# First attention, values' product: one block of 512 queries every second step in place of two halves in neighbouring steps

## The chip, the cores and the metric

One core of one Trainium2 chip runs the whole program. The metric is the device time of one execution in microseconds; three runs of the kernel before are given, and the hardware profiler took one more execution, whose trace is read below.

## What is computed

The program is a two-layer network on 16 groups of 512 tokens with 128 features. The change touches the attention of layer 0 alone:

```
x = x + proj(softmax(q k^T / sqrt(8)) v)      # 16 groups, 16 heads of 8 features, 512 tokens each
    q, k, v = split(layernorm(x) @ qkv_w + qkv_b)
```

Around it stand, in this order: the first mixture-of-experts feed-forward of layer 0 (its names begin with ffnA), this attention (att), the second feed-forward (ffnB), and layer 1 with a kernelized attention and a spline feed-forward (att1k, att1q). The attention must not start before ffnA is done, and ffnB starts when it has ended.

## The kernel before

`attn0` runs a software pipeline over 16 groups with 32 steps for each. A group has 4 units of 4 heads each, and a unit has 4 key tiles of 128 keys. Step k of the pipeline handles one key tile of one pair of heads, so that a unit takes 8 steps, and a key tile takes 2.

In every step PE, which works strictly in program order, issues up to three things:

- `again(k)`, the transposed scores "t": keys of one tile by 512 queries for two heads, two fp32r matmuls of 26 rows into one of the banks `att_pair` (L957). ACT takes the exponential of it (`exps`, L873) into `att_pt`.
- `scores(k + 43)`, the scores "s" that only serve to find the row maxima, two matmuls of 24 rows (L947). DVE reduces them (`maxed`, L698). They run 43 steps ahead of t.
- `weigh`, the product with the values "W" (L969): `att_pt` of a key tile for the four heads of the unit, against the values, into the bank `att_o`. Four fp32 matmuls stand side by side, one for each head, on 32 columns of the array each; the trace shows two instructions for each.

`att_pair` has three banks that t and s take in turn (t, s, t, s, ...). So a t must wait until DVE has reduced the s issued three uses before, and an s until ACT has taken the exponential of the t issued three uses before, which is the t of the step before. `att_pt` has 8 buffers.

`weigh` is cut into two halves of 256 queries, and the table WEIGHED says in which step of the unit (and of its follower) each half is issued: steps 4, 5, 6, 7, 8 hold one half each, step 9 two, step 10 one. Since step 8 of a unit is step 0 of the next, every block of eight steps holds: step 0 one half, 1 two, 2 one, 3 none, 4 to 7 one each.

Between the steps PE has small blocks that all go through one bank, `att_misc`: for each group one turn of the maxima (after position 2 of the 32), one of the normalized tokens (5), four of the outputs (7, 15, 25, 30), one of the finished tokens (21), and four projections (9, 13, 17, 23). Counted by position n in a group, the step number k is n - 42, so that even positions are even steps.

ACT also copies a finished unit out of `att_o` (L879, `out`), behind the exponential of the unit's step 11, which is step 3 of the next unit; the next unit's first product waits for that copy.

Of the kernel before, what the change touches and what calls it, by code (L numbers as in the profile page):

```python
# [17 lines left out]
TILES = 4  # L18
# [540 lines left out]
UNITS = 4  # L559
BLOCK = P // 4  # L560
# [2 lines left out]
LAG = STEPS + 10  # L563
SUMMED = PRODUCTS * HDIM
SHIFTED = SUMMED + 2
HALF = 256
WEIGHED = {4: ((0, 0),), 5: ((0, 1),), 6: ((1, 0),), 7: ((1, 1),), 8: ((2, 0),), 9: ((2, 1), (3, 0)), 10: ((3, 1),)}


def attn0_tensors(sb):  # L570
# [4 lines left out]
def attn0(nc, ctx, name, X, A, K, groups):  # L575
# [23 lines left out]
    vxb = mem.ring("vx", 3, [P, TILES, HEADS, BLOCK])  # L599
# [3 lines left out]
    pt = mem.ring("pt", 8, [P, 2, GROUP])  # L603
# [5 lines left out]
    misc, obank = mem.ps("misc"), mem.ps("o")  # L609
# [224 lines left out]
    def scalar(a):  # L834
        def columns(b):
            a.wait_ge(xT, b + 1)
            if b:
                a.wait_ge(vp, b)
            a.activation(xcol[:, :], misc[:, :], ACT.Copy).then_inc(xc, 1)

        def raw_q(b):
            a.wait_ge(qp, b + 1)
            if b:
                a.wait_ge(ql, b)
            a.activation(qraw[:, :], misc[:, :], ACT.Identity, bias=A["bqk"][:, 0:1]).then_inc(qr, 1)

        def raw_k(b):
            a.wait_ge(kp, b + 1)
            if b:
                a.wait_ge(kl, b)  # L850
            a.activation(kraw[:, :], misc[:, :], ACT.Identity, bias=A["bqk"][:, 1:2]).then_inc(kr, 1)

        def values(b):
            a.wait_ge(vp, b + 1)
            if b < 3:
                a.wait_ge(zeroed.sem, (1, 3, 4)[b])
            if b >= 3:
                a.wait_ge(w_, 2 * UNITS * TILES * (b - 2))
            a.activation(vxb[b % 3][:, :, :, 0:HDIM], misc[:, :].rearrange("p (t h d) -> p t h d", t=TILES, d=HDIM), ACT.Copy).then_inc(vx, 1)

        def rows(b):
            a.wait_ge(mT, b + 1)
            if b >= 2:
                a.wait_ge(wm, 16 * (b - 1))
            a.activation(mrow[b % 2][:, :], misc[:, :], ACT.Copy).then_inc(mr, 1)

        def exps(k):
            a.wait_ge(t_, k + 1)
            if k >= 8:
                a.wait_ge(w_, 2 * ((k - 8) // 2 + 1))  # L870
            if k == 0:
                a.wait_ge(fill, 32)
            a.activation(pt[k % 8][:, :, :].rearrange("p h n -> p (h n)"), pair("t", k)[:, :], ACT.Exp, scale=scale).then_inc(p_, 1)  # L873

        def out(w):
            a.wait_ge(w_, 2 * TILES * (w + 1))
            if w >= 2:
                a.wait_ge(oTT, w - 1)
            a.activation(oTb[w % 2][:, :], obank[:, :], ACT.Copy).then_inc(oT, 1)  # L879

        def final(b):
            a.wait_ge(fT, b + 1)
            if b:
                a.wait_ge(fp, b)
            a.activation(ocol[:, :], misc[:, :], ACT.Copy).then_inc(fc, 1)

        columns(0)
        raw_q(0)
        raw_k(0)
        values(0)  # L890
        for m in range(groups + 2):
            new, old, now = m + 1 < groups, m >= 2, 1 <= m <= groups
            for n in range(STEPS):
                k = STEPS * m + n - LAG
                if 0 <= k < total:
                    exps(k)
                if n == 3 and now:
                    rows(m - 1)
                if n == 5 and old:
                    out(UNITS * (m - 2) + 2)  # L900
                if n == 6 and new:
                    columns(m + 1)
                if n == 10 and new:
                    raw_q(m + 1)
                if n == 13 and old:
                    out(UNITS * (m - 2) + 3)
                if n == 14 and new:
                    raw_k(m + 1)
                if n == 18 and new:
                    values(m + 1)  # L910
                if n == 21 and now:
                    out(UNITS * (m - 1))
                if n == 22 and old:
                    final(m - 2)
                if n == 29 and now:
                    out(UNITS * (m - 1) + 1)

    def tensor(pe):
        def turned(b):
            pe.wait_ge(normed, b + 1)  # L920
            misc_free(pe, "x", b)
            turn(pe, misc, group(xn[:, :]), ident).then_inc(xT, 1)
# [6 lines left out]
        def project_k(b):  # L929
            misc_free(pe, "k", b)  # L930
            pe.matmul(misc[:, :], A["qkv"][:, C:2 * C], xcol[:, :], start=True, stop=True).then_inc(kp, 1)
# [7 lines left out]
        def scores(k):  # L939
            b, u, t, j0 = place(k)  # L940
            if k % STEPS == 0:
                pe.wait_ge(dq[b % 3], 16 * (b // 3 + 1))
                pe.wait_ge(dk[b % 3], 16 * (b // 3 + 1))
            pair_free(pe, "s", k)
            for j in (j0, j0 + 1):
                r = slice(BLOCK * j, BLOCK * j + SUMMED)
                last = pe.matmul(pair("s", k)[:, (j - j0) * 512:(j - j0 + 1) * 512], qb[b % 3][r, u, t * P:(t + 1) * P], kb[b % 3][r, u, :], start=True, stop=True)  # L947
            last.then_inc(s_, 1)

        def again(k):  # L950
            b, u, t, j0 = place(k)
            if k % STEPS == 0:
                pe.wait_ge(dm[b % 3], 64 * (b // 3 + 1))
            pair_free(pe, "t", k)
            for j in (j0, j0 + 1):
                r = slice(BLOCK * j, BLOCK * j + SHIFTED)
                last = pe.matmul(pair("t", k)[:, (j - j0) * 512:(j - j0 + 1) * 512], kb[b % 3][r, u, t * P:(t + 1) * P], qb[b % 3][r, u, :], start=True, stop=True)  # L957
            last.then_inc(t_, 1)

        def weigh(w, t, h):  # L960
            b, u = divmod(w, UNITS)
            g, cols = TILES * w + t, slice(h * HALF, (h + 1) * HALF)
            pe.wait_ge(p_, 2 * g + 2)
            if t == 0 and h == 0 and w:
                pe.wait_ge(oT, w)
            if u == 0 and t == 0 and h == 0:
                pe.wait_ge(vx, b + 1)
            for j in range(4):
                last = pe.matmul(obank[j * BLOCK:(j + 1) * BLOCK, cols], vxb[b % 3][:, t, 4 * u + j, :], pt[(2 * g + j // 2) % 8][:, j % 2, cols], start=(t, h) == (0, 0), stop=(t, h) == (TILES - 1, 1))  # L969
            last.then_inc(w_, 1)  # L970

        def maxima(b):
            pe.wait_ge(mt, b + 1)
            misc_free(pe, "maxima", b)
            for t in range(TILES):
                last = pe.transpose(misc[:, t * P:(t + 1) * P], mtb[:, t, :].bitcast(F32), ident[:, :])
            last.then_inc(mT, 1)

        def out(w):
            pe.wait_ge(oT, w + 1)  # L980
            misc_free(pe, "out", w)
            turn_back(pe, misc, oTb[w % 2], ident).then_inc(oTT, 1)
# [18 lines left out]
        for m in range(groups + 2):  # L1001
            new, old, now = m + 1 < groups, m >= 2, 1 <= m <= groups
            for n in range(STEPS):
                k = STEPS * m + n - LAG
                if 0 <= k < total:
                    again(k)
                if STEPS * m + n + 1 < total:
                    scores(STEPS * m + n + 1)
                for w in (k // 8 - 1, k // 8):
                    if 0 <= w < UNITS * groups:  # L1010
                        for t, h in WEIGHED.get(k - 8 * w, ()):
                            weigh(w, t, h)
                if n == 2 and now:
                    maxima(m - 1)
                if n == 5 and new:
                    turned(m + 1)
                if n == 7 and old:
                    out(UNITS * (m - 2) + 2)
                if n == 9 and new:
                    project_q(m + 1)  # L1020
                if n == 13 and new:
                    project_k(m + 1)
                if n == 15 and old:
                    out(UNITS * (m - 2) + 3)
                if n == 17 and new:
                    project_v(m + 1)
                if n == 21 and old:
                    final(m - 2)
                if n == 23 and old:
                    projected(m - 2)  # L1030
                if n == 25 and now:
                    out(UNITS * (m - 1))
                if n == 30 and now:
                    out(UNITS * (m - 1) + 1)
# [1514 lines left out]
```

## Time and profile before

| | us |
|---|---|
| three runs | 3387.16, 3396.52, 3408.16 |
| median | 3396.52 |
| span of the profiled execution | 3381.5 |
| first attention in it, first to last instruction, about | 443 to 1360 |

The profiled execution is one more run; the profile gives its time as the span from the first to the last instruction, 3381.5 us. That is 15.0 us under the median of the three runs and 5.7 us under the lowest. Rows of the trace are in us from the start of the span; mean durations in groups are in ns. A row of merged instructions gives the start of the first one and the time until the last one ended, so the start of the next row tells when PE went on. The granted clock (PEclk) is a share of full speed: 1.00 is 2.4 GHz, 0.50 is 1.2 GHz.

### The profile page before, as it was taken

The page shows a single profiled execution, that of the slowest core. Times are in us where ns is not written, and L with a number is a line of the kernel's source. Part 1 is how long each engine was busy: PE and PEld are TensorE (multiplying, and loading weights), DVE is VectorE, ACT ScalarE, POOL GpSimd, SP SyncE. Part 2 cuts the span into 40 slices and gives each one's busy share as a digit, 9 for nine tenths or more (in the row PEclk, how much of TensorE's full clock was granted, in tenths as well). Part 3 has the DMA queues.
Part 4 walks back from the last instruction along what each step waited for, and adds up shares of the span by engine and source line. Part 5 has one row for each costly group of instructions (what it writes and reads, how often), then busy time and mean ns, then how long its engine had stood idle before and what let it go on. Part 6 is the DMA issues. An engine that isn't in the chain of part 4 may idle for free. (4 is left out here: it accounts for less than half of the span.)

```text
span 3381.5 us, 46658 instructions
## 1 busy us (share of the span) xinstructions
PE 2992.5 (88%) x16194; PEld 1802.3 (53%) x16194; DVE 2505.1 (74%) x6050; ACT 1760.5 (52%) x2680; POOL 906.3 (27%) x885
## 2 busy tenths in 40 slices
PE   7999969999999998899995689899799999989863
PEld 5666623444444433666663456566566666656432
DVE  6878768888888871778875698967467778797765
ACT  3444406777777766344434456455344555555544
POOL 2111022121111100111101345556323333343333
PEclk9999968999999986899996589889899999999965
DMA  2000022122122110100000000000000000000000
GB/s 76 1 1 1 1 93 90 59 92 83 65 92 83 66 48 5 51 1 1 1 1 0 1 7 20 13 19 26 32 13 13 13 7 13 13 7 26 7 7 25
DMA packets 33698, 99.03 MB, mean 29 GB/s; under 512 B 4184, under 2 KB 4792, under 8 KB 29240
## 3 DMA queue, kind: packets, MB, share of 16 engines
q1 hardware_dynamic: 31288, 91.85, 7.5%
q10 hardware_dynamic: 2176, 4.19, 0.3%
q8 instruction: 130, 2.13, 0.3%
q14 instruction: 104, 0.85, 0.1%
HBM read 53.56 MB, written 42.47 MB: 28 GB/s over the span
## 5 line engine op out<-in xcount | busy, mean ns | idle before, releaser
L698 DVE TENSOR_REDUCE att_mx<-att_pair 128x2 f32<-128x1024 f32 x512 | 617.3, 1220 | 132.5 <-PE att_pair L947 132.3
L873 ACT ACTIVATE att_pt<-att_pair 128x1024 f32<-128x1024 f32 x512 | 523.0, 1025 | 241.3 <-PE att_pair L957 238.4
L969 PE MATMUL att_o<-att_pt,att_vx 128*32 128x256 f32 x4096 | 339.9, 418 | 9.9 <-ACT att_oT L879 5.1
L947 PE MATMUL att_pair<-att_k,att_q 24*128 24x512 f32 x1024 | 274.2, 539 | 48.2 <-DMA att_k<-att_spread_k 14.2
L957 PE MATMUL att_pair<-att_q,att_k 26*128 26x512 f32 x1024 | 268.0, 525 | 0.1
L957 PEld LDWEIGHTS att_pair<-att_q,att_k 26*128 26x128 f32 x1024 | 99.5, 193 | 199.0 <-issue 169.1
L449 ACT ACTIVATE ffnA_h<-ffnA_up,b 128x512 f32<-128x512 f32 x144 | 99.1, 688 | 189.4 <-PE ffnA_up L105 185.7
L449 ACT ACTIVATE ffnB_h<-ffnB_up,b 128x512 f32<-128x512 f32 x144 | 99.1, 689 | 188.4 <-PE ffnB_up L105 182.5
L947 PEld LDWEIGHTS att_pair<-att_k,att_q 24*128 24x128 f32 x1024 | 101.0, 196 | 134.4 <-ACT att_pt L873 86.9
L969 PEld LDWEIGHTS att_o<-att_pt,att_vx 128*32 128x32 f32 x4096 | 92.1, 112 | 144.6 <-issue 125.3
L1888 ACT ACTIVATE att1k_sq<-att1k_k 128x512 f32<-128x512 f32 x128 | 76.2, 595 | 162.6 <-PE att1k_k L105 162.5
L148 POOL TENSOR_TENSOR ffnB_rstd<-ffnB_rstd,minus_half 128x4 f32<-128x4 f32 x16 | 16.5, 1030 | 464.6 <-DVE ffnB_rstd L264 464.6
L1955 PE MATMUL att1k_c<-att1k_feat,att1k_xn 128*128 128x512 f32 x256 | 131.9, 642 | 7.5 <-ACT att1k_ctx L1900 7.4
L2117 DVE TENSOR_REDUCE att1q_top<-att1q_wide 128x8 f32<-128x512 f32 x128 | 87.8, 686 | 64.3 <-PE att1q_wide L105 64.1
L2410 PE MATMUL att1q_acc<-att1q_qf,att1q_mem 128*128 128x512 f32 x256 | 132.3, 598 | 3.2 <-DVE att1q_qf L2155 3.2
L517 PE MATMUL ffnA_acc<-ffnA_hc,w 128*128 128x512 f32 x256 | 130.6, 592 | 0.0
L517 PE MATMUL ffnB_acc<-ffnB_hc,w 128*128 128x512 f32 x256 | 130.5, 591 | 0.0
L103 PE MATMUL ffnA_up<-ffnA_xh,w_hi 128*128 128x512 f32 x288 | 122.4, 425 | 0.5 <-DVE ffnA_h L360 0.4
L103 PE MATMUL ffnB_up<-ffnB_xh,w_hi 128*128 128x512 f32 x288 | 121.3, 421 | 0.9 <-DVE ffnB_h L360 0.4
L2281 ACT ACTIVATE att1q_qf<-att1q_half 128x512 f32<-128x512 f32 x128 | 75.8, 596 | 81.7 <-PE att1q_half L2379 81.6
L360 DVE SCALAR_TENSOR_TENSOR ffnA_h<-ffnA_up,b,ffnA_h 128x512 f32<-128x512 f32 x144 | 107.4, 746 | 13.8 <-ACT ffnA_h L449 11.4
L360 DVE SCALAR_TENSOR_TENSOR ffnB_h<-ffnB_up,b,ffnB_h 128x512 f32<-128x512 f32 x144 | 107.4, 746 | 13.7 <-ACT ffnB_h L449 11.3
(543 smaller groups left out, 7972.7 us busy)
## 6 DMA issues: line engine op xcount, KB each, us to landing
att_q<-att_spread_q SPq DMA_DIRECT2D x16, 1024.0 KB, 5.0
att_k<-att_spread_k SPq DMA_DIRECT2D x16, 1024.0 KB, 4.8
att_spread_q<-att_qhi SPq DMA_DIRECT2D x32, 256.0 KB, 2.5
att_spread_k<-att_khi SPq DMA_DIRECT2D x32, 256.0 KB, 3.3
context<-att1k_ctx SPq DMA_DIRECT2D x16, 512.0 KB, 2.6
att1q_cin<-context SPq DMA_DIRECT2D x16, 512.0 KB, 3.3
X<-L_attn_x ACTq DMA_DIRECT2D x8, 512.0 KB, 7.9
att_spread_q<-att_qlo SPq DMA_DIRECT2D x16, 256.0 KB, 2.5
```

Of the source, the lines that this page charges most:

```text
L103: pe.matmul(out, w[0], x[0], start=start, stop=False)
L360: v.scalar_tensor_tensor(h3[n % HELD][:, :], b3[:, :], W["b13"][:, 1, c:c + 1], s1[:, :], ALU.add, ALU.mult).then_inc(S.gl, 1)
L449: a.activation(h1[n % 4][:, :], up[2 * n % 4][:, :], ACT.Silu, bias=W["b13"][:, 0, c:c + 1]).then_inc(S.sil, 1)
L517: pe.matmul(acc[:, :], W["w2"][:, c, :], src[:, :], start=False, stop=c == CHUNKS - 1).then_inc(S.dn, 1)
L698: v.tensor_reduce(top[b % 2][:, t, h:h + 2], pair("s", k)[:, :].rearrange("p (h n) -> p h n", h=2), AX, ALU.max, negate=True).then_inc(mx, 1)
L873: a.activation(pt[k % 8][:, :, :].rearrange("p h n -> p (h n)"), pair("t", k)[:, :], ACT.Exp, scale=scale).then_inc(p_, 1)
L947: last = pe.matmul(pair("s", k)[:, (j - j0) * 512:(j - j0 + 1) * 512], qb[b % 3][r, u, t * P:(t + 1) * P], kb[b % 3][r, u, :], start=True, ...
L957: last = pe.matmul(pair("t", k)[:, (j - j0) * 512:(j - j0 + 1) * 512], kb[b % 3][r, u, t * P:(t + 1) * P], qb[b % 3][r, u, :], start=True, ...
L969: last = pe.matmul(obank[j * BLOCK:(j + 1) * BLOCK, cols], vxb[b % 3][:, t, 4 * u + j, :], pt[(2 * g + j // 2) % 8][:, j % 2, cols], start ...
L1955: last = pe.matmul(cb[:, cut], group(xn[i % 4][:, :])[:, t, :], feat[i % 2][:, t, cut], start=t == 0, stop=t == TILES - 1)
L2117: v.tensor_reduce(tp[:, t, side * 8:side * 8 + 8], heads_of(wide[wide_of("g", k)][:, :]), AX, ALU.max).then_inc(top, 1)
L2410: pe.matmul(acc[:, :], memb[i % 2][:, c, :], qfb[n % 12][:, :], start=c == 0, stop=c == PAIRS - 1).then_inc(gat, 1)
```

## The change

The two halves of the product of a key tile become one block of 512 queries. The blocks stand in steps 4, 6, 8 and 10 of the unit, so in every block of eight steps the even steps hold one full block each and the odd steps none. The count that tells of finished products (`w_`) goes up once for a key tile in place of twice, and the three waits on it are halved.

```diff
-HALF = 256
-WEIGHED = {4: ((0, 0),), 5: ((0, 1),), 6: ((1, 0),), 7: ((1, 1),), 8: ((2, 0),), 9: ((2, 1), (3, 0)), 10: ((3, 1),)}
+WEIGHED = {4: 0, 6: 1, 8: 2, 10: 3}
...
-                a.wait_ge(w_, 2 * UNITS * TILES * (b - 2))
+                a.wait_ge(w_, UNITS * TILES * (b - 2))
...
-                a.wait_ge(w_, 2 * ((k - 8) // 2 + 1))
+                a.wait_ge(w_, (k - 8) // 2 + 1)
...
-            a.wait_ge(w_, 2 * TILES * (w + 1))
+            a.wait_ge(w_, TILES * (w + 1))
...
-        def weigh(w, t, h):
+        def weigh(w, t):
             b, u = divmod(w, UNITS)
-            g, cols = TILES * w + t, slice(h * HALF, (h + 1) * HALF)
+            g = TILES * w + t
             pe.wait_ge(p_, 2 * g + 2)
-            if t == 0 and h == 0 and w:
+            if t == 0 and w:
                 pe.wait_ge(oT, w)
-            if u == 0 and t == 0 and h == 0:
+            if u == 0 and t == 0:
                 pe.wait_ge(vx, b + 1)
             for j in range(4):
-                last = pe.matmul(obank[j * BLOCK:(j + 1) * BLOCK, cols], vxb[b % 3][:, t, 4 * u + j, :], pt[(2 * g + j // 2) % 8][:, j % 2, cols], start=(t, h) == (0, 0), stop=(t, h) == (TILES - 1, 1))
+                last = pe.matmul(obank[j * BLOCK:(j + 1) * BLOCK, :], vxb[b % 3][:, t, 4 * u + j, :], pt[(2 * g + j // 2) % 8][:, j % 2, :], start=t == 0, stop=t == TILES - 1)
             last.then_inc(w_, 1)
...
                 for w in (k // 8 - 1, k // 8):
-                    if 0 <= w < UNITS * groups:
-                        for t, h in WEIGHED.get(k - 8 * w, ()):
-                            weigh(w, t, h)
+                    if 0 <= w < UNITS * groups and k - 8 * w in WEIGHED:
+                        weigh(w, WEIGHED[k - 8 * w])
```

## Rows read from the trace of the kernel before

**Rows 1.** The page's shares of busy time over the whole span.

```profile
PE 2992.5 (88%) x16194; PEld 1802.3 (53%) x16194; DVE 2505.1 (74%) x6050; ACT 1760.5 (52%) x2680; POOL 906.3 (27%) x885
```

**Rows 2.** Busy time by stage: stretch, length, engines (instructions), PEclk, DMA share, GB/s.

```profile
600.00:1190.00 590.00, 570.19 (x5011) 239.62 (x5008) 494.80 (x604) 428.71 (x487) 108.92 (x118) 0.97 0.21 76
1190.00:1360.00 170.00, 153.15 (x1168) 60.99 (x1166) 73.25 (x98) 103.17 (x114) 2.29 (x3) 0.74 0.08 27
```

**Rows 3.** Costliest groups between 600 and 1200 us, by form.

```profile
L698 DVE TENSOR_REDUCE att_mx<-att_pair 128x2 f32<-128x1024 f32 x378 | 457.8, 1221 | 87.7 <-PE att_pair L947 87.7
L873 ACT ACTIVATE att_pt<-att_pair 128x1024 f32<-128x1024 f32 x378 | 386.3, 1026 | 165.2 <-PE att_pair L957 163.0
```

**Rows 4.** Timeline of PE, an ordinary pair of steps: start, us, instruction.

```profile
606.98 0.50 PE L957 MATMUL att_pair<-att_q,att_k 26*128 26x512 f32 x2
...
607.99 0.50 PE L957 MATMUL att_pair<-att_q,att_k 26*128 26x512 f32 x2
608.60 0.50 PE L947 MATMUL att_pair<-att_k,att_q 24*128 24x512 f32 x2
609.03 0.64 PE L969 MATMUL att_o<-att_pt,att_vx 128*32 128x256 f32 x8
609.60 0.50 PE L957 MATMUL att_pair<-att_q,att_k 26*128 26x512 f32 x2
```

**Rows 5.** Timeline of all engines around a step with two halves.

```profile
649.95 2.04 ACT L873 ACTIVATE att_pt<-att_pair 128x1024 f32<-128x1024 f32 x2 [1.17 <-PE att_pair L957]
...
651.03 0.50 PE L947 MATMUL att_pair<-att_k,att_q 24*128 24x512 f32 x2
...
651.46 1.07 PE L969 MATMUL att_o<-att_pt,att_vx 128*32 128x256 f32 x16
...
652.46 0.50 PE L957 MATMUL att_pair<-att_q,att_k 26*128 26x512 f32 x2
```

**Rows 6.** Timeline of PE, two of the small blocks and what follows each.

```profile
612.22 0.66 PE L976 MATMUL att_misc<-ident,att_mt 128*128 128x128 f32 x4
612.81 0.50 PE L957 MATMUL att_pair<-att_q,att_k 26*128 26x512 f32 x2
...
622.69 1.13 PE L927 MATMUL att_misc<-att_xcol,aqkv 128*128 128x512 f32 x2
623.75 0.50 PE L957 MATMUL att_pair<-att_q,att_k 26*128 26x512 f32 x2
```

**Rows 7.** Busy time by group, eleven in a row, from one turn of maxima to the next.

```profile
662.10:711.90 49.80, 48.03 (x436) 20.30 (x432) 42.24 (x53) 36.94 (x42) 9.23 (x10) 1.00 0.22 81
711.90:762.70 50.80, 49.19 (x436) 20.77 (x432) 42.67 (x52) 36.38 (x42) 9.23 (x10) 0.97 0.23 80
762.70:815.10 52.40, 50.82 (x437) 21.18 (x433) 44.32 (x54) 37.56 (x43) 9.23 (x10) 0.92 0.21 78
815.10:867.10 52.00, 50.19 (x437) 20.90 (x433) 41.91 (x53) 36.93 (x42) 9.23 (x10) 0.95 0.21 78
...
sum 561.90, PE 543.48 PEld 228.71 DVE 469.06 ACT 406.18 POOL 96.12; mean PE 49.41 PEld 20.79 DVE 42.64 ACT 36.93 POOL 8.74
```

**Rows 8.** Busy time of two short stretches, before and after the clock fell.

```profile
752.20:755.60 3.40, 2.95 (x28) 1.21 (x28) 3.11 (x9) 2.92 (x4) 1.03 (x1) 1.00 0.00 0
755.60:759.00 3.40, 3.40 (x26) 1.28 (x18) 2.58 (x4) 1.49 (x2) 3.26 (x5) 0.50 0.00 0
```

**Rows 9.** Timeline of PE just before the clock fell.

```profile
754.77 0.50 PE L947 MATMUL att_pair<-att_k,att_q 24*128 24x512 f32 x2 [0.26 <-ACT att_pt L873]
755.35 0.87 PE L969 MATMUL att_o<-att_pt,att_vx 128*32 128x256 f32 x8
```

**Rows 10.** Timeline at the attention's end: t and products alone, clock at 0.50.

```profile
1296.46 0.79 PE L957 MATMUL att_pair<-att_q,att_k 26*128 26x512 f32 x2
...
1298.19 0.79 PE L957 MATMUL att_pair<-att_q,att_k 26*128 26x512 f32 x2
...
1300.78 0.79 PE L957 MATMUL att_pair<-att_q,att_k 26*128 26x512 f32 x2
```

## The prediction

> **What bounds the kernel now.** I read the page first. PE is busy 88% of the span, DVE 74% [rows 1]; that says little of this stage, because the end of a matmul is modelled and a waiting matmul looks busy. The stage is the first attention. In its middle PE shows 570.19 of 590.00 us busy, DVE 494.80 and ACT 428.71 [rows 2]. The groups give the unit prices: a reduction 1.22 us and an exponential 1.03 us for each step [rows 3]. By group of 32 steps, an undisturbed one takes 49.80 us, in which DVE is busy 42.24 and ACT 36.94 [rows 7]: nobody but PE looks full. So the timeline of PE decides. In an ordinary pair of steps t starts at 606.98 (s with it), the next t at 607.99, its s only at 608.60, the product at 609.03, and the next pair at 609.60 [rows 4]: 2.62 us for two steps. The s of the odd step is 0.61 us behind its own t. The reader is to see why in the other timeline: two exponentials run from 649.95 for 2.04 us, and the odd step's s starts at 651.03, when the first of them has ended [rows 5]. Three banks in turn mean that an s waits for the exponential of the t before. So the pair is a chain, not a sum of PE's work:
>
> t to the next step's s, through the exponential: 608.60 - 606.98 = 1.62 us
> s to its product: 609.03 - 608.60 = 0.43
> half product until PE goes on: 609.60 - 609.03 = 0.57
> together 2.62, as measured.
>
> The half product of the even step lies in the shade of the exponential (0.43 + 0.57 + 0.43 = 1.43 of 1.62 us). Only the odd step's half is on the chain. That is the point on which everything hangs.
>
> **The change part by part.**
>
> *Block size.* A step with two halves runs its products from 651.46 to 652.46 [rows 5]: 1.00 us, where two separate halves take 2 x 0.57 = 1.14. A full block streams the same columns in half as many instructions, so I take 1.00. The nearest other row with 512 columns, a projection in one piece, keeps PE from 622.69 to 623.75, 1.06 us [rows 6]; that is the upper bound. Below 1.00 I take 0.97 as the bound, should the fewer instructions save anything. A 0.03 us saving on 16 blocks in 16 groups would be 8 us, 0.06 more would be 15 us.
>
> *Cadence.* Now the full block stands behind the even s, and nothing behind the odd one. With the even s at 0: block at 0.43, odd t at 1.43. The odd s needs the even t's exponential, which was started early: at 1.62 at the latest. The next even s needs the exponential of the odd t: 1.43 + 1.62 = 3.05. The chain is now odd t, exponential, even s, full block: 1.62 + 0.43 + 1.00 = 3.05 us for two steps, 0.43 more than before. The block of the odd step has left the chain (it was 0.57), and a block of 1.00 has come on it. The half that used the shade of the exponential is gone from there. 16 pairs: 48.80 us for a group.
>
> *The step without a product and the copy of the unit.* The even step 4 waits for the copy of the last unit. Before, s at 754.77 and product at 755.35 lie 0.58 apart in place of 0.43 [rows 9]. The exponential ahead of the copy is the chain's own, so this stays: 4 units x 0.15 = 0.6 us.
>
> *Small blocks.* Nine of the eleven stand behind odd steps, two behind even ones. A turn keeps PE 0.59 us (612.22 to 612.81), a projection 1.06 [rows 6]. Before, those behind odd steps are on the chain. After the change the odd s is at 1.62, PE is free at 2.05, and the even s can't start before 3.05: room for 1.0 us. Five turns vanish in it; four projections stick out by some 0.06 to 0.1, together 0.3. The two behind even steps stand on the chain: 2 x 0.59 = 1.2. This cover is the gain of the change: seven turns and four projections, 7 x 0.59 + 4 x 1.06 = 8.4 us of the 49.80, were mostly paid before. If the cover fails, the five and the four cost 5 x 0.59 + 4 x 1.06 = 7.2 us a group.
>
> *Sum for a group at full clock.* 48.80 + 0.6 + 0.3 + 1.2 = 50.9 against 49.80: +1.1, in 15.5 groups' worth of steps +17 us. DVE needs 42.24 and ACT 36.94 of it, so neither becomes the bound. Extra work of ACT behind an exponential (0.6 us) moves an odd s, not the odd t.
>
> *The other waits.* The first exponential that needs a product's buffer back comes four steps after the even block, more than the longest wait. A product needs exponentials three steps old. Both cost nothing. The wait on `oT` above is the only one with something queued: the next t and s.
>
> *End of the stage.* With t and products alone a step with one half takes 1298.19 - 1296.46 = 1.73 us at half clock and one with two halves 1300.78 - 1298.19 = 2.59 [rows 10]. A unit before: six of 1.73, one of 2.59, one without a product at ACT's 1.03, 14.0 us. After: four of 2.59 and four that are a bare t, 0.72 by PE (1.73 less the half product, 1.02 by its modelled end), 13.2. Five units: -4 us.
>
> *The clock.* Here is the term that decides. Group rows differ: 49.80 at clock 1.00, then 50.80 at 0.97, 52.40 at 0.92, 52.00 at 0.95, and eleven groups take 561.90 us [rows 7], where 11 x 49.80 would be 547.8. The 14.1 us are what low clock costs now, in six falls: four short ones as the one shown (0.50 from 755.60 to 759.00 [rows 8]), two that each spread over two groups. A fall's mean price is 14.1 / 6 = 2.35 us. In the stretch before the fall, 752.20 to 755.60, PE issued 28 matmuls [rows 8], s waited for its exponential with PE idle 0.26 us, and only then came the next product [rows 9]: it is the one step of a group's 32 that has neither a product nor a small block behind it. Finer stretches of the same view put the other five falls at this same step (one stands here for all): 0.55 falls for a bare step, in 11 groups. After the change there are seven bare steps in a group (positions 1, 3, 11, 19, 27, 29, 31) and PE waits a microsecond at each. They make three places: 11, 19, and a run of five. At 0.55 a place 1.65 falls, and the run is long enough for more than one, so I take 2.1 a group. Less certain than the rest: a full block beside each bare step speaks against a fall, fewer matmuls per microsecond for it. 2.1 x 2.35 = 4.9 us, less the 1.3 (14.1 / 11) that are paid already, is +3.6 a group, +56 in 15.5. Bounds: 0 falls, -20; 4 falls (one in half the bare steps) 9.4 - 1.3, +126.
>
> The Trainium skill, "TensorE: Matmul & The Clock Gate", section "HAM oscillation — how this bites in real kernels", names long gaps without any matmul as what throttles PE. By that rule alone no fall would come here and the time would be the clock-holds rival below. The trace speaks against the rule as the only cause: the clock fell with no gap over 0.26 us near it [rows 9]. The same page's section on a second failure mode, short idles between groups of matmuls, is what the row looks like.
>
> *Rest of the kernel.* It isn't touched. I give it ±10 us for clock patterns that shift.
>
> **Sum.** Cadence +17, end -4, clock +56: I forecast +60 after rounding down for the doubts on the run of five. On the profiled span 3381.5 + 60 = 3441.5; the median lies 15.0 above the span, so 3456.5, said as 3456.
>
> **Rivals.**
>
> A, *the clock holds*, or falls no oftener than now: +17 - 4 = +13, 3410. For it: each pair still has a full product, and the bare step that falls now has less product near it. Against: five bare steps in a row, where one is enough in half the groups. Decides below 0.7 falls a group.
>
> B, *faster*: fewer product blocks. Eight steps hold seven blocks now and four afterwards, and two halves in one block save 1.14 - 1.00 = 0.14 us [rows 4, 5]: 192 blocks fewer x 0.14 = 27 us, still within 1%. To get over 1%, the small blocks must vanish and the pair must stay under 2.8 us, which wants an exponential chain of 1.4 in place of 1.62: 0.25 x 16 x 16 = 64 us less than my cadence gives, 13 - 64, about 3345. It decides from a pair of 2.9 us down. Against it: two rows agree on 1.62, to 0.01. The Trainium skill, "TensorEngine Tiling (Array Packing)", says in "Key Properties" that a change of tiling mode drains the engine, which speaks for this rival: fewer changes. The 0.14 us are this kernel's price of it, and it isn't on the chain.
>
> C, *the clock stays low for long stretches*: four falls a group, +17 - 4 + 126 = +139, 3535. For it: at half clock the gaps shrink, so PE looks busier and the clock should come back, which speaks against.
>
> D, *the change does nothing*, if a block of 512 were cut in two again: the projection row shows 512 columns in one piece with the same two instructions for each fp32 product that a half has [rows 6, 4]. Then the order still changes and the result is near mine. No chance of its own.
>
> **How the numbers follow.** Forecast (1 to 3.3 falls a group, +30 to +100): 0.63. A: 0.24. C: 0.05. B: 0.08. About 1% (34 us) is what a measurement of this kernel can tell from no change. Slower by over 1% holds nearly all of the forecast and C, 0.67; same holds A and a little of the others, 0.25; faster 0.08. The range takes in A's lower part and the forecast's upper: 3398 to 3496. The bounds of the block size (-8, +15) and of the rest (±10) lie inside it. The forecast's own range is 3427 to 3496.
>
> **What would show it.** In the profile after: 2048 products of 512 columns; pairs of 3.05 us with t at 1.43 and the even s last, released by the exponential; small blocks behind odd steps that cost nothing; a group at clock 1.00, if there is one, of 50.9; and the granted clock in the middle of the attention at 0.85 to 0.93, against 0.97 [rows 2]. I am wrong if undisturbed groups take under 50 or over 52 us, if the clock there stays at 0.97, or if ffnB and later move by over 10 us.

## The result and the profile after

The changed kernel takes 3439.0 us in the median (3426.68 to 3445.6), the kernel before 3391.84 (3372.02 to 3408.16): ratio 1.0162, 95% interval 1.012 to 1.0204. It is slower: by 47.2 us by the two medians, by some 55 us by the ratio, and in either case by more than 1%; whether by 2% the interval leaves open. The profiled execution took 3443.13 us for a span of 3441.2, so only 1.9 us lie around the span; the two spans differ by 3441.2 - 3381.5 = 59.7 us.

The first rows are the page's busy line and the middle of the attention by stage (stretch, length, busy us of PE, PE's loads, DVE, ACT, POOL, then the granted clock), which answer to [rows 1, 2]:

```profile
PE 2987.5 (87%) x14146; PEld 1756.8 (51%) x14146; DVE 2505.1 (73%) x6050; ACT 1754.5 (51%) x2680; POOL 904.7 (26%) x885
```

```profile
600.00:1190.00 590.00, 529.80 (x3236) 195.16 (x3232) 454.76 (x557) 390.37 (x445) 97.39 (x106) 0.86 0.20 73
```

There are 16194 - 14146 = 2048 matmuls fewer and the stage still takes longer: the granted clock of the middle went from 0.97 to 0.86. The cadence shows in PE's timeline, at full clock:

```profile
660.12 1.06 PE L968 MATMUL att_o<-att_pt,att_vx 128*32 128x512 f32 x8
661.12 0.50 PE L956 MATMUL att_pair<-att_q,att_k 26*128 26x512 f32 x2
661.21 0.50 PE L946 MATMUL att_pair<-att_k,att_q 24*128 24x512 f32 x2
661.55 0.46 PE L956 MATMUL att_pair<-att_q,att_k 26*128 26x512 f32 x2
662.73 0.50 PE L946 MATMUL att_pair<-att_k,att_q 24*128 24x512 f32 x2 [0.72 <-ACT att_pt L872]
663.17 1.07 PE L968 MATMUL att_o<-att_pt,att_vx 128*32 128x512 f32 x8
664.16 0.50 PE L956 MATMUL att_pair<-att_q,att_k 26*128 26x512 f32 x2
...
664.60 0.66 PE L111 MATMUL att_misc<-ident,att_otok 128*128 128x128 f32 x4
```

Block to block 663.17 - 660.12 = 3.05 us, where a pair took 2.62 [rows 4]. The even s (662.73) waits for the exponential of the odd t (661.12), and PE idles 0.72 us. The even t (661.55) was issued long before, but it doesn't fill the gap. In the next pair a turn of tokens (664.60) stands in that gap and costs nothing.

The groups, to be held against [rows 7]. No group among eleven is without a stretch of half clock; one of the two shortest and one of the longest:

```profile
688.40:740.00 51.60, 45.58 (x304) 17.27 (x304) 43.31 (x52) 36.89 (x42) 9.21 (x10) 0.96 0.22 78
848.90:907.20 58.30, 53.00 (x306) 19.03 (x304) 42.80 (x52) 36.90 (x42) 9.19 (x10) 0.79 0.19 70
```

Half clock lasts 2 x (1 - clock) x length: 4.1 us in the first, 24.5 in the second. So a microsecond at half clock costs (58.3 - 51.6) / (24.5 - 4.1) = 0.33 us, and a group at full clock would take about 51.6 - 4.1 x 0.33 = 50.25. That is an estimate, since the clock has only two digits here; fill_narrow, below, has groups at full clock of the same order of work, and they take 50.43. One fall, before and after it, as in [rows 8]:

```profile
674.70:678.10 3.40, 2.32 (x16) 0.72 (x16) 3.01 (x8) 2.29 (x4) 0.71 (x1) 1.00 0.00 0
678.10:681.50 3.40, 3.40 (x14) 1.20 (x14) 1.56 (x2) 1.35 (x2) 3.29 (x5) 0.51 0.02 5
```

PE is busy 2.32 of 3.40 us ahead of it, with 16 matmuls, where it was 2.95 with 28 before.

To split the stage I take it from the first product to the last, and the length of half clock in it from the trace's record of the clock, which is finer than the two digits of the rows:

```profile
532.60:1349.10 816.50, 784.71 (x6749) 325.53 (x6746) 621.45 (x753) 581.14 (x655) 121.94 (x132) 0.93 0.19 69
```

```profile
533.70:1408.30 874.60, 779.92 (x4702) 282.58 (x4698) 623.70 (x753) 576.64 (x655) 121.45 (x132) 0.85 0.18 64
```

Before 816.5 us with 120.7 at half clock, after 874.6 with 263.6: the stage is 58.1 us longer of the spans' 59.7. At 0.34 us for a microsecond of half clock (from the experiment fill_before, below) the rest is 775.5 before and 784.9 after. So **cadence +9.4 us, clock +48.6 us**.

That is one trace of each kernel. For every execution the span and the mean granted clock of the whole program were taken too, and 2 x (1 - clock) x span is the half clock in it. It differs from execution to execution of one kernel, and so does the time: over 22, 13 and 20 executions of the kernel before, a microsecond more of half clock goes with 0.33, 0.34 and 0.38 us more time, which is the price above once more. The means:

| kernel | executions | half clock in the whole program, us |
|---|---|---|
| before | 55 | 619 |
| changed | 4 | 749 |
| halves_even | 7 | 675 |
| fill_after | 10 | 601 |
| fill_before | 10 | 577 |
| fill_narrow | 4 | 716 |
| exp_even | 10 | 590 |
| pad1 | 6 | 651 |
| one_each | 5 | 519 |

The changed kernel has 130 us more of it than the kernel before, at 0.34 us each 44 us of the 55.

### The profile page after: what moved, and what is told of

Same layout as the page of the kernel before. It is cut to its first block and busy times, and to the rows that moved or that the text cites. A ratio compares the mean times of both kernels' runs of the same rounds, so it can differ in the third digit from the quotient of the medians.

```text
span 3441.2 us, 42562 instructions
## 1 busy us (share of the span) xinstructions
PE 2987.5 (87%) x14146; PEld 1756.8 (51%) x14146; DVE 2505.1 (73%) x6050; ACT 1754.5 (51%) x2680; POOL 904.7 (26%) x885
## 5 line engine op out<-in xcount | busy, mean ns | idle before, releaser
L872 ACT ACTIVATE att_pt<-att_pair 128x1024 f32<-128x1024 f32 x512 | 514.5, 1025 | 303.3 <-PE att_pair L956 300.9
L946 PE MATMUL att_pair<-att_k,att_q 24*128 24x512 f32 x1024 | 292.3, 575 | 105.8 <-ACT att_pt L872 76.8
L968 PE MATMUL att_o<-att_pt,att_vx 128*32 128x512 f32 x2048 | 323.7, 709 | 12.3 <-ACT att_oT L878 7.5
L956 PE MATMUL att_pair<-att_q,att_k 26*128 26x512 f32 x1024 | 258.2, 537 | 1.6 <-DVE att_mx L697 1.5
L1820 DVE TENSOR_REDUCE att1k_diag<-att1k_sq 128x16 f32<-128x1024 f32 x64 | 77.4, 1209 | 52.5 <-ACT att1k_sq L1886 52.4
```

The costliest lines, as they stand in the source:

```text
L968: last = pe.matmul(obank[j * BLOCK:(j + 1) * BLOCK, :], vxb[b % 3][:, t, 4 * u + j, :], pt[(2 * g + j // 2) % 8][:, j % 2, :], start=t == ...
```

## The experiments

All are judged by the ratio to the kernel before and by this split. "Rest" is the length from first to last product less 0.34 x the half clock in it. A row that starts at 532 to 535 us is that stretch of the run named.

**halves_even: the place without the width.**

```diff
 # on the kernel before
-WEIGHED = {4: ((0, 0),), 5: ((0, 1),), 6: ((1, 0),), 7: ((1, 1),), 8: ((2, 0),), 9: ((2, 1), (3, 0)), 10: ((3, 1),)}
+WEIGHED = {4: ((0, 0), (0, 1)), 6: ((1, 0), (1, 1)), 8: ((2, 0), (2, 1)), 10: ((3, 0), (3, 1))}
```

> Two halves of 256 queries stand one behind the other in each even step, so the placement is the changed kernel's and the width is not. My theory (the place of the product on the chain t, exponential, s, product sets the cadence, and the waits it makes let the clock fall): the same time as the changed kernel, 3439 +- 10 us, about 1.016 of the kernel before; pairs of 3.05 us at full clock. Rival (the 512-column block itself is what is slower or faster): the time would stay near the kernel before, 3392 us.

```profile
533.50:1373.00 839.50, 741.80 (x6750) 347.13 (x6746) 623.91 (x753) 576.97 (x655) 121.67 (x132) 0.91 0.18 67
```

3416.0 us, ratio 1.0077 (1.0044 to 1.011). Rest 839.4 - 0.34 x 154.5 = 786.9, the changed kernel's 784.9 to 2 us: the width of the block is worth nothing in the cadence, the place makes it. But the ratio lies midway between my two numbers: half clock is 154.5 us, not 263.6. The clock falls as often, eleven times from 664 to 1200 us and in the same run of bare steps, but a fall lasts 9.3 us in the mean, where the changed kernel's last 13.3. Something else sets how long the clock is low.

**block_odd: the block where the small blocks are.**

```diff
-WEIGHED = {4: 0, 6: 1, 8: 2, 10: 3}
+WEIGHED = {5: 0, 7: 1, 9: 2, 11: 3}
```

> The blocks of 512 queries stand in steps 5, 7, 9 and 11 of the unit, so always in odd steps, where nine of the eleven small blocks of a group stand too. My theory: the pair's chain is still 3.05 us, but the small blocks behind odd steps now lie on it; a group at full clock takes 50.3 (measured after the change, with the low clock taken out) plus 5 x 0.59 + 4 x 1.06 less what the two behind even steps give back, 1.2, so about 56.3 us; in 15.5 groups +93 us on a changed kernel at full clock. PE has fewer gaps, so fewer falls give back at most 60 us. Expected 3470 to 3530. Rival (the cover of small blocks is worth nothing, PE's work only adds up): the same as the changed kernel, 3439.

```profile
534.00:1483.80 949.80, 779.51 (x4695) 278.86 (x4694) 631.77 (x752) 572.07 (x653) 121.48 (x132) 0.86 0.16 59
```

3520.21 us, ratio 1.0402 (1.0357 to 1.0446). Two groups in a row take 122.86 us with 30.7 of half clock, so one at full clock (122.86 - 0.34 x 30.7) / 2 = 56.2 us, where 56.3 was expected. The cover over nine small blocks is real, worth 56.2 - 50.4 = 5.8 us a group, net of the two blocks that are now covered. PE's timeline at full clock has the prices by themselves: a bare pair takes 3.05 us from block to block (735.90 to 738.95), one with a turn behind the block 3.63 (738.95 to 742.58), one with a projection 4.14 (742.58 to 746.72).

**fill_after: work in the gaps.** FILLED are the even positions behind a bare odd step; the repeats write the same values into the same bank.

```diff
+FILL, FILLED = 3, (0, 2, 4, 12, 20, 28, 30)
...
         def again(k):
...
-            for j in (j0, j0 + 1):
+            for j in (j0, j0 + 1) * (1 + FILL * ((k + LAG) % STEPS in FILLED)):
```

> The changed kernel, in which the even step's t behind a bare odd step (seven in a group) is computed four times into the same bank, so PE works where it waited for the exponential; the results are the same, and the repeats lie in the 1.0 us gap, off the chain. My theory (the clock falls because of those gaps): the granted clock of the attention's middle goes from 0.86 to 0.95 or more, and the time falls by 40 to 60 us of the changed kernel's loss, to 3380 to 3405. Rival (the falls have another cause, or the cadence alone is the loss): more work on PE, so the same time or slower, 3439 to 3470, and the clock stays at 0.86.

```profile
534.40:1366.10 831.70, 796.26 (x5368) 324.47 (x5364) 630.09 (x753) 584.53 (x655) 121.80 (x132) 0.93 0.19 68
600.00:1190.00 590.00, 569.84 (x3928) 236.27 (x3926) 491.04 (x591) 422.33 (x476) 101.49 (x110) 0.97 0.22 80
```

3396.73 us, ratio 1.0033 (1.001 to 1.0056): more work, 42 us less time. Half clock fell from 263.6 to 115.6 us, and the clock of the middle, the second row, went from 0.86 to 0.97, as my theory asked. The filler isn't quite free: a group at full clock takes 50.8 us in place of 50.43, rest 792.4. So this run fills the gaps and moves everything in time as well, and pad1, below, shows what a move in time can do by itself.

**fill_before: the same in the one bare step of the kernel before.**

```diff
+FILL, FILLED = 1, (30,)
...
-            for j in (j0, j0 + 1):
+            for j in (j0, j0 + 1) * (1 + FILL * ((k + LAG) % STEPS in FILLED)):
```

> The kernel before, in which the t behind its one bare step (position 30 of a group) is computed twice. My theory: all six falls in the attention's middle stood behind that step, and they cost 14.1 us in eleven groups; with the gap filled they go, so the middle's clock is 1.00 in place of 0.97, and the time is 10 to 20 us under the kernel before, a ratio of 0.994 to 0.997. Rival (the falls there have another cause): no difference, clock 0.97.

```profile
533.90:1329.40 795.50, 765.81 (x6782) 320.11 (x6778) 616.28 (x753) 580.57 (x655) 121.88 (x132) 0.96 0.19 71
```

3371.07 us, ratio 0.9965 (0.9941 to 0.9989). Thirteen groups in a row take 49.84 us each, what the undisturbed groups of the kernel before take, so nothing is moved in time, and no fall is left there; the kernel before has six in eleven groups. Half clock went from 120.7 to 58.9 us and the stretch from 816.5 to 795.5: 21.0 / 61.8 = 0.34 us for one, the price used above.

**quarters_even and fill_narrow: do instructions and loads count?** Quarters cut each block of the changed kernel in four of 128 queries in the same step; the narrow filler puts six matmuls of 32 columns where fill_after had six of 512.

```diff
 # quarters_even
+            for c in range(4):
+                cols = slice(c * P, (c + 1) * P)
+                for j in range(4):
+                    last = pe.matmul(obank[j * BLOCK:(j + 1) * BLOCK, cols], vxb[b % 3][:, t, 4 * u + j, :], pt[(2 * g + j // 2) % 8][:, j % 2, cols], start=(t, c) == (0, 0), stop=(t, c) == (TILES - 1, 3))
 # fill_narrow, in again(k)
+            if (k + LAG) % STEPS in FILLED:
+                for j in (j0, j0 + 1) * 3:
+                    r = slice(BLOCK * j, BLOCK * j + SHIFTED)
+                    last = pe.matmul(pair("t", k)[:, (j - j0) * 512:(j - j0) * 512 + 32], kb[b % 3][r, u, t * P:(t + 1) * P], qb[b % 3][r, u, 0:32], start=True, stop=True)
```

> The changed kernel with each block of 512 queries cut in four of 128, all in the same even step. The two halves in one step gave 1.0077, the block of 512 1.0162, with the same pairs of 3.05 us and the same block of 1.00 us, but 105.8 against 194.6 us of low clock in the attention's middle. Theory L: the number of instructions and weight loads counts toward what keeps the clock up, so four quarters give still less low clock, under 80 us, and a ratio of 1.000 to 1.006, as long as the block still takes 1.00 us; each 0.1 us that it takes more costs 0.1 x 256 = 26 us. Theory P: the falls of halves and blocks differ only by where they happened to lie, and quarters can land on either side, 1.006 to 1.018, with 100 to 200 us of low clock.

> The changed kernel with filler of another kind in the same gaps (the even step's t behind a bare odd step): six more matmuls of 32 columns into the same bank, each with its load of 128 weight columns, in place of six of 512 columns. Theory L (loads and instructions count): the clock comes back as with the wide filler, low clock in the middle near its 72 us, ratio near its 1.0033. Theory S (the streamed columns count): 6 x 32 columns are nothing, so low clock stays near 195 us and the ratio near 1.016.

The row is a group of fill_narrow at full clock.

```profile
851.30:901.70 50.40, 45.84 (x350) 19.68 (x346) 43.18 (x53) 36.84 (x43) 9.22 (x10) 1.00 0.22 81
```

Quarters 3411.54, 1.0096 (1.0063 to 1.0128); narrow filler 3428.15, 1.0137 (1.011 to 1.0164). The stage takes 833.3 and 847.1 us with 134.5 and 184.8 us of half clock. Quarters have twice the instructions of halves and no better time, so L's ratio of 1.006 at most failed, and up to 1200 us, the middle of these expectations, half clock is 92 us, over L's 80 and under P's 100. The narrow filler took 79 us of half clock away in this trace, but not the 148 of the wide one, and its ratio can't be told from the changed kernel's (1.012 to 1.0204); over the whole program its executions have 716 us of half clock against 749 and 601. So L failed here too, and S is neither borne out nor refuted.

**exp_odd and exp_even: which exponential is the chain?**

```diff
+    extra = mem.ring("extra", 4, [P, 256])
...
+            if k % 2 == 1:      # 0 in exp_even
+                a.activation(extra[k // 2 % 4][:, :], pair("t", k)[:, 0:256], ACT.Exp, scale=scale)
             a.activation(pt[k % 8][:, :, :].rearrange("p h n -> p (h n)"), pair("t", k)[:, :], ACT.Exp, scale=scale).then_inc(p_, 1)
```

> The changed kernel, in which ACT also takes the exponential of the first 256 columns into a spare buffer, before the real one, for odd steps only: some 0.37 us more (half of a 512-column copy's 0.59, with its fixed part). My theory: the odd step's exponential is on the chain of the pair, so every pair grows by it: 256 x 0.37 = 95 us, less what ACT's own work behind hides, and more low clock on top: 3520 to 3570. Rival (PE's own work or the throughput of ACT sets the pace): the same as exp_even.

> The same extra exponential, for even steps only. My theory: the even step's exponential runs in the slack while PE does the full block, 3.05 - 2 x 1.03 us of ACT's pair, so most of the 0.37 us is hidden: 0 to 0.15 us a pair, 3439 to 3480. Rival (throughput): the same as exp_odd.

```profile
1238.20:1299.60 61.40, 52.51 (x308) 18.71 (x304) 43.34 (x52) 40.83 (x58) 9.19 (x10) 0.83 0.18 66
```

```profile
732.40:783.70 51.30, 45.63 (x311) 17.68 (x304) 43.26 (x53) 40.99 (x59) 9.21 (x10) 1.00 0.22 79
```

The rows are one group of each. ACT does the same extra work in both (40.83 and 40.99 us). Odd: 3588.5 us, 1.0604 (1.0569 to 1.0639); a group 61.4 with 20.5 of half clock, 54.4 without, 4.0 more than 50.43. Even: 3400.1 us, 1.0043 (1.0021 to 1.0065); a group 51.3, 0.9 more. So the odd exponential is the chain and throughput of ACT isn't the limit. The odd one costs 4.0 / 16 = 0.25 us a pair, not the 0.38 that its row lasts, because the exponential behind it starts before that row ends: 0.28 us after it in exp_odd (median of 256) and 0.26 in exp_even. And exp_even, with more to do, is 39 us faster than the changed kernel: its half clock is 78.3 us.

**pad1 and pad3: is it a matter of where a gap lies in time?** The same extra exponential in one, or in three, odd steps of a group.

```diff
-            if k % 2 == 1:
+            if (k + LAG) % STEPS in (19,):      # (11, 19, 27) in pad3
```

> The changed kernel with one extra exponential of 256 columns (0.38 us) in a group, ahead of the real one in the odd step of position 19, so on the chain: every group gets 0.38 us longer and nothing else changes, 16 x 0.38 = +6 us. Theory P (whether a gap lets the clock fall depends on where it happens to lie in time, which the length of the group moves on): low clock between the first and the last product changes by over 40 us from the changed kernel's 263.6, either way, and the time with it by over 10 us beyond the 6. Theory W (the width of the block or the number of loads sets the falls): low clock stays within 30 us of 263.6 and the time is 3445 +- 8.

> The same in three odd steps, positions 11, 19 and 27: 1.14 us a group, +18 us, which makes the group at full clock 51.4 us, near the 51.34 of exp_even, where twelve groups ran without a fall. Theory P: low clock drops far below 263.6, to under 150 us, and the time to 3400 to 3430 though ACT has more to do on the chain. Theory W: low clock stays, 3457 +- 8.

```profile
532.40:1364.00 831.60, 728.62 (x4699) 270.29 (x4698) 630.47 (x753) 582.48 (x671) 121.83 (x132) 0.93 0.19 68
```

```profile
752.55 0.38 ACT L874 ACTIVATE att_extra<-att_pair 128x256 f32<-128x256 f32 x1
752.83 1.94 ACT L875 ACTIVATE att_pt<-att_pair 128x1024 f32<-128x1024 f32 x2
...
753.90 0.50 PE L949 MATMUL att_pair<-att_k,att_q 24*128 24x512 f32 x2 [1.00 <-ACT att_pt L875]
```

pad1: 3408.38 us, 1.0073 (1.0043 to 1.0103), 31 us faster than the changed kernel with more on the chain of every group. What is added is 0.28 us, not 0.38: the real exponential starts at 752.83, 0.28 after the extra one, and PE's gap at 753.90 is 1.00 us in place of 0.72. Half clock is 123.0 us in place of 263.6; seven of its groups are at clock 1.00 and take 50.71, which is 50.43 without the pad. And the gap that was made longer now draws falls: of the six from 634 to 1238 us, four (at 754.4, 856.8, 1119.7 and 1174.3) begin within 2 us behind this padded wait, where the changed kernel has none. pad3: 3438.07, 1.0168 (1.0115 to 1.022), the stage 881.1 us with 246.1 of half clock: my 3400 to 3430 failed, though five groups in a row of 51.25 us ran without a fall, in a trace that had falls ahead of them and behind. So W is out, and P holds in its first half: a small shift in time cuts half clock by more than a factor of two in these traces, and over the whole program from 749 to 651 us in the mean of the executions. Which length of a group is good I could not say ahead.

**one_each: no bare step and no double one, by order alone.**

```diff
 # on the kernel before
-WEIGHED = {4: ((0, 0),), 5: ((0, 1),), 6: ((1, 0),), 7: ((1, 1),), 8: ((2, 0),), 9: ((2, 1), (3, 0)), 10: ((3, 1),)}
+WEIGHED = {4: ((0, 0),), 5: ((0, 1),), 6: ((1, 0),), 7: ((1, 1),), 8: ((2, 0),), 9: ((2, 1),), 10: ((3, 0),), 11: ((3, 1),)}
```

> The kernel before with the odd half moved: one half of 256 queries in each of the steps 4 to 11 of the unit, so no step holds two and none is bare. At full clock a pair is 2.62 us everywhere: the double step gives back 0.43, the once bare step pays 0.57, and the copy of the unit now ends later, behind a product, which delays the next unit's first product by some 0.3: 0.3 to 0.5 us a unit, +1 to +2 us a group, +15 to +30 us; no falls in the middle give back 14 x 15.5 / 11 = 20. Expected 3380 to 3405. Rival (bare steps have nothing to do with the falls): low clock stays at 0.97 in the middle, 3405 to 3425.

```profile
532.40:1316.00 783.60, 753.75 (x6750) 305.83 (x6746) 616.61 (x753) 583.95 (x655) 122.35 (x132) 0.99 0.20 72
```

3354.42 us, 0.9921 (0.9869 to 0.9973): faster than both kernels, and than I expected. A group costs 50.5 in place of 49.84, 0.65 more where I had reckoned with 1 to 2, and the rest is 780.6, +5 where I had +15 to +30. And half clock is gone from the stage, all but 8.8 us at its start, also from its end, where I had counted on nothing.

**fill_tail: the filler at the stage's end too.**

```diff
-            for j in (j0, j0 + 1) * (1 + FILL * ((k + LAG) % STEPS in FILLED)):
+            for j in (j0, j0 + 1) * (1 + FILL * ((k + LAG) % STEPS in FILLED or k + LAG + 1 >= total)):
```

> The kernel before with its bare step's t computed twice, as in fill_before, and in the stage's last 42 steps, where no s is left, every t computed twice. fill_before had 58.9 us of low clock left, all in this end. If the repeats keep the clock up there, 58.9 x 0.34 = 20 us come back, less what they cost when PE sets the pace: up to 42 x 0.2 = 8 us. Expected 5 to 15 us under fill_before, a ratio of 0.991 to 0.995. Rival (each t repeated only lengthens PE's queue): 0.9965 to 0.999.

```profile
1263.40:1351.90 88.50, 83.48 (x491) 31.53 (x484) 3.43 (x11) 38.47 (x41) 0.00 (x0) 0.50 0.01 1
```

3400.64 us, 1.0061 (1.0037 to 1.0085): a miss, and its premise was wrong in part. Of fill_before's 58.9 us of half clock only 30.7 lie behind the last s (1260.9); 27.3 lie from 1217.4 on, where s still runs. In fill_tail's end the clock fell once, at 1263.4, and stayed at 0.50 for the whole end. From the last reduction to the last product fill_before takes 68.5 us and fill_tail 100.7, some 0.75 us more for each repeated t, about what a bare t keeps PE at half clock (0.72 in the prediction): there they cost in full. One fall is back in its middle as well (at 754.8), where fill_before had none.

## Why the prediction was right

*Pair of 3.05 us.* As worked out: 3.05 in the timeline, and exp_odd against exp_even shows which exponential carries it (4.0 against 0.9 us a group).

*Block of 1.00 us.* 660.12 to 661.12; halves_even, quarters_even and the changed kernel have the same rest to 3 us (786.9, 787.5, 784.9). The bounds of 0.97 and 1.06 weren't needed.

*Small blocks are covered.* Shown by block_odd: a group comes to 56.2 us where 56.3 was expected.

*Group at full clock, 50.9.* It is 50.43, in fill_narrow as it stands and in pad1 less 0.28: the term was 0.5 too large. In such a group of fill_narrow ten of the sixteen pairs take 3.05 us from block to block, the four with the copy of a unit 0.10 to 0.15 more, where 0.15 was taken, and the two with a turn on the chain 3.63, as the 0.59 taken. The projections stick out by nothing, where I had 0.3: that is the term that was too large; the rest is rounding of 3.05. With it cadence and end came to +9.4 in place of +17 - 4 = +13; the end wasn't measured apart.

*Clock, +56.* 48.6 measured. That it comes from the gaps is shown best by fill_before, where nothing but the one gap changed and six falls in eleven groups went to none, though fill_tail, with the same middle, has one fall there; by one_each, which has no bare step and no fall in its middle; and by pad1, where the gap made longer draws the falls. fill_after alone wouldn't show it: its 148 us of half clock less are hardly more than the 140.6 that pad1 took away with every gap left in place. Over the executions it is 148 against 98, so filling does more than shifting, but part of its effect can be the shift.

The two factors of the term were off against each other. I had 2.1 falls a group at 2.35 us. There are 11 in the eleven groups from 634.4 to 1238.4, one a group, with a mean length of 13.3 us, so 13.3 x 0.34 = 4.5 us each. They all stand in the run of five bare steps that goes over the group's end; the lone bare steps at 11 and 19 have none. So the place was named too widely, and the length, which I took from the kernel before (6.8 us on average), was too short. And pad1 shows that the term isn't a property of this order of work alone: 0.28 us more a group took 0.34 x 140.6 = 48 us of it away in the two traces, all there was, and 0.34 x 98 = 33 us in the mean of the executions, two thirds. The size of my forecast was partly luck; +10 to +60 would have been honest for this step.

*The sum.* +60 on the spans, and the spans differ by 59.7: with the executions of one kernel up to 46 us apart (the kernel before from 3360.87 to 3407.27) and two factors that made up for each other, the agreement to 0.3 us is luck. The median is 3439.0 and not 3456, mostly because I added 15.0 us for the distance of the median from the span. That distance was no constant: 1.9 us lie around the span, and the rest was that the profiled execution had been faster than the three runs given.

*Rivals.* A (clock holds, 3410) isn't what happened, but the same order of work with another timing comes to it (pad1 3408, exp_even 3400). B needed a pair under 2.9 us. C needed four falls a group.

*The Trainium skill.* "TensorE: Matmul & The Clock Gate" names long gaps as what takes the clock back. Here the clock fell at 678.1 with no gap over 0.72 us in the 18 us before. Its section on the second failure mode, short idles between groups of matmuls, is nearer to what the runs show.

*What stays open.* Why the block of 512 draws 263.6 us of half clock and the two halves 154.5 at the same cadence. pad1 moves the number as much with a shift of 0.28 us, so the width need not be the cause; no run holds the timing fixed and changes the width alone. What share of fill_after's gain is the filling and what the shift, and whether narrow filler gives back anything at all, are open too.

## What to carry to other kernels

Where an engine waits on a ring of few banks, write the chain between two uses of a bank out in order of time, and ask of each block that is moved whether it lies in the chain or in its shade: merging two halves saved 0.14 us of PE and cost 0.43, since one half had been free. Then look for steps of PE with nothing behind them. Here gaps of 0.7 us that cost nothing by themselves had the clock halved for 13 us at a time in the mean, at 0.34 us each; an even spread (one_each) or a repeated matmul in the gap brought 0.8% and 0.35% on the kernel before. The price of a microsecond at half clock held from run to run; how many of them a trace has is a draw, so test it with a pad of a few tenths of a microsecond before a gain or a loss is put down to a change.

## What the runs showed of the hardware that was not expected

- Added work made the kernel faster three times: fill_after by 42 us, exp_even by 39, pad1 by 31 against the changed kernel, each with half clock of 115.6, 78.3 and 123.0 us in place of 263.6.
- A PE that is kept busy at half clock doesn't get the full clock back for that alone: fill_tail's PE shows 83.48 of 88.50 us busy, all at 0.50.
- Half clock costs this stage 0.34 us a microsecond (21.0 / 61.8), less than the half that work on PE alone would lose. ACT and DVE keep their speed: an exponential takes 1.02 us and a reduction 1.22 at half clock too (exp_odd, 722 to 724 us). That they hide the rest is argued and not shown.
- Two exponentials in a row on ACT overlap: one of 256 columns lasts 0.38 us, but the next starts 0.26 to 0.28 us after it.
